# Second attention of a four-layer kernel: softmax sums and their inverse change layout by DMA through DRAM, the output's two halves are joined by DMA, and the out projection takes two passes

## The reference

```python
q, k, v = jnp.split(x @ w_attn + b_attn, 3, axis=-1)      # 16 heads of 16
att = jnp.einsum('bhqd,bhkd->bhqk', q, k) / 4
att = softmax(where(causal, att, -inf), axis=-1)
y = jnp.einsum('bhqk,bhkd->bhqd', att, v)
return y @ w_proj + b_proj
```

## Time and profile before

| | |
|---|---|
| median of 3 runs | 2306.89 us (2301.71 to 2308.46) |
| the profiled execution | 2301.61 us, of which span 2299.9 us |
| PE busy | 2141.7 us (93% of the span) |
| DVE busy | 1507.0 us (66%) |
| ACT busy | 1176.5 us (51%) |
| POOL busy | 541.1 us (24%) |
| DMA, its main queue | 36.83 MB, 6.1% of 16 engines |

### The profile page before, as it was taken

The page is one execution under the profiler, slowest core; times in us unless marked ns, Lnnn a source line. Parts: engine busy times, 40 slices in busy tenths (PEclk is TensorE's granted clock), DMA queues, the critical chain, the costliest instruction groups (busy, mean ns, idle before and its releaser), DMA issues. The chain is left out here.

```text
span 2299.9 us, 36921 instructions
## 1 busy us (share of the span) xinstructions
PE 2141.7 (93%) x12776; PEld 1731.9 (75%) x12776; DVE 1507.0 (66%) x2657; ACT 1176.5 (51%) x2137; POOL 541.1 (24%) x543
## 2 busy tenths in 40 slices
PE   4999999999999999999999979977999987999996
PEld 3888888888888888888888868754555544888885
DVE  4766676676676666767667765456766664566665
ACT  3654565464465555546546555436655664333333
POOL 3012021031031021021020116213434343233332
PEclk8999999999999999999999999988999986899998
DMA  3010010010010010010020010000000000000001
GB/s 79 1 40 2 1 40 2 1 40 2 1 40 2 1 40 2 1 40 2 14 54 1 10 65 10 1 10 3 3 6 3 1 1 21 15 28 21 21 21 37
DMA packets 36811, 39.13 MB, mean 17 GB/s; under 512 B 7712, under 2 KB 33184, under 8 KB 36640
## 3 DMA queue, kind: packets, MB, share of 16 engines
q1 hardware_dynamic: 36640, 36.83, 6.1%
HBM read 34.71 MB, written 2.10 MB: 16 GB/s over the span
## 5 line engine op out<-in xcount | busy, mean ns | idle before, releaser
L735 ACT ACTIVATE attn_probT_hi<-psum 128x512 fp32r<-128x512 f32 x512 | 278.2, 595 | 305.5 <-PE psum L621 305.5
L777 DVE TENSOR_REDUCE attn_neg_max<-psum 128x1 f32<-128x1024 f32 x256 | 313.3, 1224 | 180.1 <-PE psum L81 179.2
L823 DVE TENSOR_TENSOR attn_probT_lo<-psum,attn_probT_hi 128x512 fp32r<-128x512 f32 x512 | 327.6, 682 | 37.7 <-ACT attn_probT_hi L735 37.7
L714 ACT ACTIVATE attn_prob<-psum,attn_neg_max 128x1024 f32<-128x1024 f32 x256 | 286.8, 1120 | 7.2 <-DVE attn_neg_max L777 7.2
L621 PE MATMUL psum<-ident_sb,attn_prob 128*128 128x128 f32 x2048 | 266.7, 273 | 22.0 <-ACT attn_prob L714 12.7
L621 PEld LDWEIGHTS psum<-ident_sb,attn_prob 128*128 128x128 f32 x2048 | 237.1, 140 | 63.2 <-DVE attn_probT_lo L823 13.3
L552 POOL TENSOR_TENSOR attn_v_lo<-x_sb,attn_v_hi 128x512 fp32r<-128x512 f32 x64 | 82.0, 1281 | 766.9 <-ACT attn_v_hi L743 766.9
L2023 ACT ACTIVATE attn_probT<-psum 128x512 f32<-128x512 f32 (+3 forms) x384 | 166.0, 488 | 130.8 <-PE psum L1936 125.9
L81 PE MATMUL psum<-attn_probT_hi,attn_v_hi 128*128 128x512 f32 x512 | 212.2, 414 | 0.6 <-DVE attn_probT_lo L823 0.6
L81 PE MATMUL psum<-attn_key_hi,attn_q_hi 128*128 128x512 f32 x512 | 201.1, 393 | 0.3 <-DVE attn_key_lo L809 0.2
L81 PE MATMUL psum<-attn_probT_lo,attn_v_hi 128*128 128x512 f32 x512 | 201.2, 393 | 0.0
(11 more groups left out here) (207 smaller groups left out, 4888.5 us busy)
## 6 DMA issues: line engine op xcount, KB each, us to landing
moe_staged<-in_moe_w SPq DMA_DIRECT2D x18, 384.0 KB, 3.0
acc_sb<-in_x SPq DMA_DIRECT2D x4, 512.0 KB, 5.3
x_sb<-in_wq_codes SPq DMA_DIRECT2D x8, 256.0 KB, 2.7
x_sb<-in_wq_scales SPq DMA_DIRECT2D x32, 64.0 KB, 3.0
x_sb<-in_wk_codes SPq DMA_DIRECT2D x8, 256.0 KB, 4.0
x_sb<-in_wk_scales SPq DMA_DIRECT2D x32, 64.0 KB, 4.6
x_sb<-in_wv_codes SPq DMA_DIRECT2D x8, 256.0 KB, 4.9
x_sb<-in_wv_scales SPq DMA_DIRECT2D x32, 64.0 KB, 5.6
```

The source lines that it names most:

```text
L714: nc.scalar.activation(prob[:, i % 2, :], scores(i).rearrange("p a b -> p (a b)"), ACT.Exp, bias=neg_max[:, i % 2:i % 2 + 1], accum_out=to ...
L735: nc.scalar.activation(probT[0][:, g % 2, half_tile * GT:(half_tile + 1) * GT, j * P:(j + 1) * P], ring(use).rearrange("p (t n) -> p t n", ...
L777: nc.vector.tensor_reduce(neg_max[:, i % 2:i % 2 + 1], scores(i), AX.XY, ALU.max, negate=True).then_inc(max_ready, 1)
L823: nc.vector.tensor_tensor(to[1], ring(use).rearrange("p (t n) -> p t n", n=P), f32(to[0]), ALU.subtract).then_inc(ring_free, 1)
```

## The change

The sum rows of `o` go by DMA to DRAM and come back with queries along partitions; DVE takes the reciprocal; the inverse goes to DRAM and comes back repeated over the 32 rows of each head. PE's sums and spread, POOL's widening and ACT's copy are gone. `make_y` runs its three instructions in one step, r = 3 or r = 7. `y` now holds the rounded part in rows 0 to 15 of each head, and four DMAs put the rest, from `y_lo`, into rows 16 to 31; the projection weights stand twice in the 32 rows, so that two passes (with the hi and the lo of the weights) do what three did. DVE's reciprocal stands at r = 1 and r = 5. The steps behind the last quad are 8.

```diff
-    LEAD, FIRST, TAIL = 10, 4, 10
+    LEAD, FIRST, TAIL = 10, 4, 8
...
-        1: [("stack", 1, 0, 2), ("stack", 1, 0, 3), ("sums", -1, 1, 0)],
+        1: [("stack", 1, 0, 2), ("stack", 1, 0, 3)],
...
-        3: [("project", 1, 1, 0), ("spread", -1, 1, 0)],
+        3: [("project", 1, 1, 0)],
...
-        5: [("stack", 1, 1, 2), ("stack", 1, 1, 3), ("sums", 0, 0, 0)],
+        5: [("stack", 1, 1, 2), ("stack", 1, 1, 3)],
...
-        7: [("out", -1, 1, 1), ("spread", 0, 0, 0)],
+        7: [("out", -1, 1, 1)],
...
-    Y_AFTER = {(1, 3): 0, (1, 4): 1, (1, 5): 2, (0, 7): 0, (0, 8): 1, (0, 9): 2}
+    INVERT_AT, Y_AT = {1: (1, 1), 5: (0, 0)}, {3: (1, 1), 7: (0, 0)}
...
+            def move_sums(half, c):
+                at = half * chunks + c
+                sp.wait_ge(o_done, at + 1)
+                sp.dma_start(sums_row[c:c + 1].squeeze(0), o[D1:P:HEAD_ROWS, c, :]).then_inc(sums_moved, 16)
+                sp.wait_ge(sums_moved, 64 * at + 16)
+                sp.dma_start(sums[:, c, :], sums_row[c:c + 1].squeeze(0).rearrange("h (p n) -> (h p) n", n=GT * HG)).then_inc(sums_moved, 16)
+            def move_inverse(half, c):
+                at = half * chunks + c
+                sp.wait_ge(inverted, at + 1)
+                sp.dma_start(inverse_row[c:c + 1].squeeze(0).rearrange("h (p n) -> (h p) n", n=GT * HG), inverse[:, c, :]).then_inc(sums_moved, 16)
+                sp.wait_ge(sums_moved, 64 * at + 48)
+                sp.dma_start(over_sum[:, c, :], inverse_row[c:c + 1].squeeze(0).unsqueeze(1).broadcast_to([HG, HEAD_ROWS, NB])).then_inc(sums_moved, 16)
+            def move_lo(half, c):
+                sp.wait_ge(y_split, 3 * (half * chunks + c + 1))
+                for h in range(HG):
+                    at = h * HEAD_ROWS
+                    sp.dma_start(f32(y[at + D1:at + 2 * D1, c, :]), f32(y_lo[at:at + D1, :])).then_inc(y_ready, 16)
+            for half in range(1, 3):
+                next_weights(half)
+            for half in range(HALVES + 1):
+                if half:
+                    move_sums(half - 1, 1)
+                    move_inverse(half - 1, 1)
+                    move_lo(half - 1, 1)
+                if half < HALVES:
+                    move_sums(half, 0)
+                    move_inverse(half, 0)
+                    next_weights(half + 3)
+                    move_lo(half, 0)
...
+            def make_y(of, c):
+                before_this = of * chunks + c
+                pool.wait_ge(sums_moved, 64 * (before_this + 1))
+                nc.gpsimd.tensor_tensor(y_whole[:], o[:, c, :], over_sum[:, c, :], ALU.mult).then_inc(y_split, 1)
+                if of:
+                    pool.wait_ge(misc_full, last_out[before_this - chunks] + 1)
+                pool.wait_ge(y_split, 3 * before_this + 1)
+                nc.gpsimd.tensor_tensor(y[:, c, :], y_whole[:], one[:].broadcast_to([P, NB]), ALU.mult).then_inc(y_split, 1)
+                if before_this:
+                    pool.wait_ge(y_ready, before_this * HG * 16)
+                pool.wait_ge(y_split, 3 * before_this + 2)
+                nc.gpsimd.tensor_tensor(y_lo[:], y_whole[:], f32(y[:, c, :]), ALU.subtract).then_inc(y_split, 1)
...
-                        pe.wait_ge(y_ready, at + 1)
+                        pe.wait_ge(y_ready, (at + 1) * HG * 16)
...
-                            mm = three_passes(nc, misc[:, j * C:(j + 1) * C], [x[:, t * P:(t + 1) * P] for x in y],
-                                              [x[:, of % passes, :] for x in wp])
+                            for half_of in range(2):
+                                mm = nc.tensor.matmul(misc[:, j * C:(j + 1) * C], y[:, c, t * P:(t + 1) * P],
+                                                      wp[half_of][:, of % passes, :], start=half_of == 0, stop=half_of == 1)
...
+            def invert(of, c):
+                dve.wait_ge(sums_moved, 64 * (of * chunks + c) + 32)
+                nc.vector.reciprocal(inverse[:, c, :], sums[:, c, :]).then_inc(inverted, 1)
...
-    w_proj = np.pad(w_proj, [(0, 0), (0, 0), (0, HEAD_ROWS - D1), (0, 0)])
+    w_proj = np.concatenate([w_proj, w_proj], axis=2)
```

More of the change, by code:

```diff
@@ L1795, in attention1_stage @@
         o = st.sb("o", [P, chunks, NB])
[L1796 to L1799, removed]
+        sums, inverse = (st.sb(n, [P, chunks, GT * HG]) for n in ("sums", "inverse"))
+        over_sum = st.sb("over_sum", [P, chunks, NB])
+        sums_row, inverse_row = (nc.dram_tensor(f"{name}_{n}", (chunks, HG, NB), F32).ap() for n in ("sums_row", "inverse_row"))
+        y_whole, y_lo = st.sb("y_whole", [P, NB]), st.sb("y_lo", [P, NB], F32R)
+        y = st.sb("y", [P, chunks, NB], F32R)
         misc_free = [st.sem(f"misc_free{n}") for n in range(RING)]
@@ L1889, in step @@
                     split_weights(pool, half + 2)
-                for (c, quad), n in Y_AFTER.items():
-                    of = half - c
-                    if r == quad and 0 <= of < HALVES:
-                        make_y(of, c, n)
-                for kind, of, c, n in jobs(g):
-                    if kind == "sums":
-                        pool.wait_ge(inverted, of * chunks + c + 1)
-                        nc.gpsimd.tensor_tensor(wide[:], over_sum[:].unsqueeze(2).broadcast_to([P, GT * HG, HEAD_ROWS]),
-                                                one[:].unsqueeze(2).broadcast_to([P, GT * HG, HEAD_ROWS]), ALU.mult).then_inc(widened, 1)
+                if r in Y_AT and 0 <= half - Y_AT[r][0] < HALVES:
+                    make_y(half - Y_AT[r][0], Y_AT[r][1])
                 if g in X_ACC_DVE:
@@ L2053, in step @@
                         before.take_hi(act, of, misc_bank(use).unsqueeze(1), (part,))
-                    if kind == "spread":
-                        act.wait_ge(misc_full, use + 1)
-                        nc.scalar.activation(factor, misc_bank(use), ACT.Copy).then_inc(spread_done, 1)
-                        act.wait_ge(spread_done, of * chunks + c + 1)
-                        act.nop().then_inc(small_free(use), 1)
                 if g in X_ACC_ACT:
@@ L2091, in small @@
                         take_v(of, part, use)
-                    elif kind == "sums":
-                        dve.wait_ge(misc_full, use + 1)
-                        nc.vector.reciprocal(over_sum[:], misc[:, 0:GT * HG]).then_inc(inverted, 1)
-                        dve.wait_ge(inverted, at + 1)
-                        dve.nop().then_inc(small_free(use), 1)
                     elif kind == "out":
@@ L2119, in step @@
                 small(g)
+                if g % QUADS in INVERT_AT and 0 <= g // QUADS - INVERT_AT[g % QUADS][0] < HALVES:
+                    invert(g // QUADS - INVERT_AT[g % QUADS][0], INVERT_AT[g % QUADS][1])
                 if g in X_ACC_DVE:
```

44 lines of the change are left out of this document (8 added, 36 removed).

## The result

The changed kernel took 2311.28 us (median of 18 runs); the kernel before, run beside it, 2307.97 (18 runs). The ratio is 1.0023 (95% interval 1.0014 to 1.0033): 3 to 8 us **slower**, where 7 us less was forecast. One of the 18 executions of the changed kernel took 11453 us, at a granted clock of 1.00; the ratio leaves it out, and what delayed it no run shows. The profiled execution took 2309.37 us, span 2307.7.

What follows compares the result with a forecast made beforehand. PE was taken to set the pace, except where it waits for chains through ACT or POOL. Terms -14.1 (half-passes 1 to 6), -0.5, -1.2 and +8.8 sum to -7.0 us: 2300 against the median 2306.9, range 2290 to 2316.

Steps and rivals of the forecast that it cites:

- the outer two: Half-passes 0 and 7: gains of 0.5 us (out jobs alone) and 1.2 us (parts of out and sums).
- the end: After the last chunk's copy, nothing covers the transfers: 18.0 us instead of 8.4 to the first out matmul, net loss 8.8.
- the broadcast: Load of the inverse repeated over 32 rows, 256 KB: taken as 4.0 us, in place at 1771.0 for chunk 0.
- the one at quad 9: POOL's selects queue behind undivided make_y; quad 9's product starts at 1775.55, before 1775.50, so PE's 1.9 us are lost.
- the sums at r = 5: Removing them from PE lets it reach quad 9 0.88 us earlier, where it meets POOL.
- spread at r = 7: Removing its transposes lets PE reach quad 9 up to 0.53 us earlier, where it meets POOL.
- 0.77 at r = 3: Without ACT's copy to `wide`, quad 4's product starts earlier: gain 0.60 + 0.17 us per half-pass.
- the wait at r = 10: PE's 1.15 us wait for `y_lo` at out goes, since the rest is joined at 1778.2: gain 1.1.
- Rival 1: Broadcast load runs on four DMA engines, 5.7 us, 1.7 more per half-pass and at the end: 2312 us; chance 0.25.
- Rival 2: Small transfers through DRAM land late, 3.0 us each and the broadcast 5.0: total +10, 2317 us; chance 0.14.
- Rival 3: Clock: fewer slow stretches in six half-passes give 2292 us, or more give 2316; chance 0.14 faster, 0.04 slower.
- Rival 4: PE's removed work is covered everywhere, also at r = 3 and 10; only the end remains, +9 at worst; 0.05 with mixtures.

Runs made afterwards that it cites:

- e4: Changed kernel with the last of 16 chunks by the way of the kernel before (sums and spread on PE, three passes, no transfer); 2307.07 us, ratio 0.9997.
- e5: Changed kernel with PE's sums matmuls put back at r = 1 and r = 5, their result unused; 2319.51 us, ratio 1.0051 to the kernel before.
- e3: Changed kernel with the store of chunk 0's sums ahead of the previous chunk's y_lo transfers on SP's queue; 2307.12 us, ratio 1.0008 to the kernel before.
- e7: Changed kernel with the broadcast of the inverse as four transfers of 32 partitions each; 2304.63 us, ratio 0.9992 to the kernel before.
- e2: Changed kernel with chunk 0's make_y split over r = 7 and 8 and both its out projections at r = 11; 2300.11 us, ratio 0.9961.
- e6: Kernel before with only the joined y, two-pass out projection, make_y split, chunk 0's outs at r = 11; sums and spread stay on PE; 2302.38 us, ratio 0.9979.
- e11: The changed kernel itself, unedited, measured again beside the kernel before; 2315.45 us, ratio 1.0030.

## Why the prediction was wrong

The sum was -14.1 for half-passes 1 to 6, -1.7 for the outer two, +8.8 for the end. **The end was right**: 18.2 us for 18.0, +8.9 and +8.5 for +8.8 (e4 takes it back). Inside it, errors cancelled: small transfers took 1.4 to 1.7 us from issue to the next step (forecast 2.1), the broadcast 5.3 to the start of POOL's product (4.1), the four of `y_lo` 3.9 (3.4, since an issue took 0.61, not 0.43). That the total came within 0.2 is in part luck. The prediction's "No row shows a store or load this small" is wrong, for the list of DMA issues of before has loads smaller than 8 KB:

```profile
attn_bias_in<-in_b_qk SPq DMA_DIRECT2D x8, 0.5 KB, 2.4
```

With 2.4 in place of 2.0 each of the three small transfers would have been 0.4 longer in the sum, where they measured less than 2.0.

**The step that failed is the one at quad 9**: "POOL is free at 1770.9 ... quad 9's product starts at 1775.55". In the frame of the kernel before (4.52 later) it started at 1777.13, 1.6 late, made of two terms, in this order:

- **0.88 for the sums at r = 5.** The prediction let POOL's selects come 1.12 earlier "by the sums and one out job". It had seen that the sums at r = 1 only fill a wait for ACT's keys, and did not ask the same of r = 5, where before no wait was visible because the sums filled it. Quad 6 did not move (e5). Only the out job moved the selects, by 0.24.
- **0.70 for the broadcast.** It was forecast at 1771.0, and landed in that frame at 1772.5. Two causes: on SP the store of the sums stands behind `move_lo` of the chunk before, which cost 1.3 (e3), and the transfer took 5.0, not 4.1; the store of the inverse gave 0.7 back. This term is there in half-passes 4 to 6 alone. And the two are no independent sum: had the selects come when forecast, POOL would have waited for the broadcast up to about the same 1772.5. The prediction counted what the SP queue delays behind `move_inverse`, but not `move_lo`.

With e3's or e7's edit quad 9 starts at 19.82, with e2's at 18.49. The transposes of spread at r = 7 (0.53) brought nothing at quad 9 either: PE waits 0.29 for POOL's select at quad 8, in front of which they ran (1767.31 above), and in e6, which still has sums and spread on PE, quads 8 and 9 come within 0.14 us of e2's. So of the 1.89 us that PE "would be" earlier at quad 9 only the two out jobs were to be had, 0.46 in e2, with the block out of the way. The block did not use up a gain of 1.9; it cost more than the gain that was there.

Half-passes 1 to 6 fell by 12.1 us once the block was split, so the terms that the sum went by were near their size: 0.77 at r = 3, the wait at r = 10 (in four half-passes, not six), 0.24 per out job. Of the 12.6 us between the forecast's 14.1 and the 1.5 measured, quad 9 has 8.1; the low clock below has a part in the rest, but how much no run separates. The prediction named the place and the engine, and called the price zero because old gain and new loss came out equal there; an equality to 0.05 us between two chains is no result to rest a sum on.

**Rival 1** (broadcast on few engines) is borne out in its mechanism: a share of 0.21, 5.3 us where the rival had 5.7, and more share in less time when the outermost dimension was split (e7). The engines themselves were not counted. The Trainium skill's rule on the number of engines (DMA: Bandwidth & Descriptors, "Why a DMA increments its semaphore by 16 and not by 1") gives four here; the trace agrees with its 0.21 of 16 engines, which is the time of 3.4. The rival's price, 1.7 in each half-pass, was too high, since only 0.7 to 1.1 us reached POOL, in three of the six. Its total of +4.9 lies near the measured 3 to 8, partly by luck. **Rival 2** (small transfers late) is false: they were faster than taken. **Rival 3** (the clock) has a part, on the slow side. In half-passes 4 to 6 before, the clock was low in quads 2 to 3; after, it was low behind the new wait at quad 9. Window of the changed kernel over quads 10 and 11:

```profile
1774.00:1784.00 10.00, 9.42 (x53) 5.51 (x52) 5.90 (x10) 3.56 (x10) 3.00 (x6) 0.51 0.03 7
```

Over the 12 runs of e11 the mean granted clock was 0.950, over the kernel before's beside them 0.957. Part of that is the longer end, where PE idles at 0.50 and loses nothing; the rest costs, as the 5.8 us between the two executions of the changed kernel show. **Rival 4** is false at r = 3 and r = 10, but true for the sums and for the spread at r = 7.

Of what should be seen: quad 4 came earlier by 0.77, the wait for the keys, no wait at out, and 18 us at the end were there. At quad 9 the wait was 2.0 to 2.4 in half-passes 4 to 6, just under the 2.5 that I had given as the sign of failure; that sign was set too wide.

## What to carry to other kernels

Where PE looks busy without a gap, ask at every place what it would wait for if the work in front of it were gone: a wait that is exactly filled shows no row. When steps are merged into one on an engine that also serves short urgent work, count what queues behind the longest block, since that, not the engine's busy share, here a third, is the price; here cutting the block in two, with out a step later, was worth 14 us. And put transfers that start a chain ahead of those that end one on the same queue: here that was 1.3 us of the chain, though too little in time to be clear of noise.

## What the runs showed of the hardware

- A transfer of 8 KB to or from DRAM took less than forecast: the store of the sums 1.70 us from issue to the next issue, the store of the inverse 1.41, the load back 1.67 to its reader. In the kernel before loads of 0.5 KB had a median of 2.4 from issue to landing, those of 128 KB 2.0. The Trainium skill gives a fixed part of about 2.0 us, measured on GpSimd's path (DMA: Bandwidth & Descriptors, "Anatomy of one DMA — SWDGE (gpsimd) path"); these, issued by SP, lie below it.
- 256 KB repeated over rows took 5.3 us as one transfer at a share of 0.21 and 3.3 us as four at 0.36, though their issue alone takes 1.7.
- Four issues from SBUF to SBUF took 2.44 us, 0.61 each, where one of a small load took 0.43.
- Two executions of one kernel, with the same instructions in half-passes 1 to 6, differed by 4.0 us there: PE was busy 5.8 us longer at the lower clock (0.90 for 0.93) and idle 1.8 less. An edit worth less than that shows in the timeline's offsets, not in one execution's time.
